# Stacked rows of keys and queries moved in longer and shorter pieces through scratches with gaps, in a cross-attention and sparse-gate kernel on one core

## What is computed

```python
q = (Q @ Wq.T + bq).reshape(B, S, H, D_H).transpose(0, 2, 1, 3)
k = (K @ Wk.T + bk).reshape(B, S, H, D_H).transpose(0, 2, 1, 3)
scores = jnp.einsum('bhqd,bhkd->bhqk', q, k) * inv_sqrt_dh
attn = jax.nn.softmax(scores, axis=-1)
ctx = jnp.einsum('bhqk,bhkd->bhqd', attn, v)
x = x + (ctx.transpose(0, 2, 1, 3).reshape(B, S, D_K) @ Wo.T + bo)   # then x = x + the sparse layer of layernorm(x)
```

## Time and profile before

| | |
|---|---|
| median of three runs | 531.14 us |
| the profiled execution's own time | 530.78 us |
| its span in the profile | 529.0 us |
| outside the span | 1.8 us |
| PE busy over the span | 393.7 us (74%) |
| DVE busy over the span | 411.9 us (78%) |
| DMA queue q1 (SP's), share of the 16 engines over the span | 40.3% |
| packets, and bytes moved | 138970, 53.02 MB |

### The profile page before, as it was taken

The page is one execution under the profiler, slowest core; times in us unless marked ns, Lnnn a source line. Parts: engine busy times, 40 slices in busy tenths (PEclk is TensorE's granted clock), DMA queues, the critical chain, the costliest instruction groups (busy, mean ns, idle before and its releaser), DMA issues.

```text
span 529.0 us, 16337 instructions
## 1 busy us (share of the span) xinstructions
PE 393.7 (74%) x5502; PEld 306.8 (58%) x5516; DVE 411.9 (78%) x1941; ACT 393.8 (74%) x1069; POOL 361.0 (68%) x514
## 2 busy tenths in 40 slices
PE   3455989999999999999897435766685685586543
PEld 1124677777877787777785224555574564465442
DVE  7555566767776877677764299999999999999946
ACT  3414667877887788786675568889999999999863
POOL 7356766788786777865211202569999999989996
PEclk9999988999999999999999556697769768878865
DMA  5787788778878887777500000000000000000011
GB/s 156 160 210 180 164 204 204 182 196 203 186 177 188 189 208 188 188 176 179 124 7 2 0 0 2 1 1 22 22 20 20 22 21 22 21 22 20 22 39 60
DMA packets 138970, 53.02 MB, mean 100 GB/s; under 512 B 105146, under 2 KB 131195, under 8 KB 137339
## 3 DMA queue, kind: packets, MB, share of 16 engines
q1 hardware_dynamic: 136712, 51.47, 40.3%
q10 hardware_dynamic: 2176, 0.52, 0.5%
HBM read 34.67 MB, written 16.78 MB: 97 GB/s over the span
## 4 chain that ended last, share of the span: by engine, by line
SPq 30%; DVE 27%; PE 11%; ACT 9%; DMA 9%; issue 6%; POOL 6%; DVEq 0%; POOLq 0%; ACTq 0%
SPq L295 27%; DVE tops L1050 11%; DVE kst L1062 11%; DMA k_scratch<-k_parts 6%; ACT kst L775 3%; SPq L280 2%; DMA qst<-q_scratch 2%; PE ps_pv L355 2%; POOL kst L1229 1%; ACT kst L786 1%; PE ps_row L530 1%; PE ps_col L340 1%; PE ps_col L530 1%; ACT kst L823 1%; PE ps_row L384 1%
## 5 line engine op out<-in xcount | busy, mean ns | idle before, releaser
L900 DVE TENSOR_REDUCE m<-ps_row 128x8 f32<-128x512 f32 x128 | 82.3, 685 | 53.1 <-PE ps_row L384 53.1
L646 ACT ACTIVATE pT<-ps_col 128x512 f32<-128x512 f32 x128 | 68.6, 588 | 30.3 <-PE ps_col L340 30.3
L1050 DVE MAX8 tops<-kst 128x8 f32<-128x128 f32 x384 | 78.5, 265 | 0.0
L355 PE MATMUL ps_pv<-vx,pT 128*64 128x18 f32 x2048 | 72.8, 213 | 0.0
L355 PEld LDWEIGHTS ps_pv<-vx,pT 128*64 128x64 f32 x2048 | 66.4, 139 | 6.9 <-ACT pT L646 3.5
L1062 DVE MATCH_REPLACE8 kst<-tops,kst 128x128 f32<-128x128 f32 x264 | 69.0, 266 | 0.0
L384 PE MATMUL ps_row<-kst,qst 96*64 96x128 bf16 x1024 | 41.6, 224 | 11.0 <-DMA qst<-q_scratch 11.0
L340 PEld LDWEIGHTS ps_col<-qst,kst 100*128 100x128 bf16 x1024 | 33.9, 99 | 23.9 <-issue 11.5
L340 PE MATMUL ps_col<-qst,kst 100*128 100x64 bf16 x1024 | 41.6, 195 | 7.1 <-DMA qst<-mT 7.1
L558 PE MATMUL ps_pv<-idb,kst 128*128 128x128 bf16 x120 | 10.9, 243 | 42.3 <-ACT kst L786 42.1
L384 PEld LDWEIGHTS ps_row<-kst,qst 96*64 96x64 bf16 x1024 | 32.5, 113 | 14.8 <-DMA qst<-q_scratch 13.1
(11 more groups left out here) (157 smaller groups left out, 1256.3 us busy)
## 6 DMA issues: line engine op xcount, KB each, us to landing
k_scratch<-k_parts SPq DMA_DIRECT2D x32, 192.0 KB, 3.0
q_scratch<-q_parts SPq DMA_DIRECT2D x32, 192.0 KB, 3.0
kst<-k_scratch SPq DMA_DIRECT2D x32, 192.0 KB
qst<-q_scratch SPq DMA_DIRECT2D x32, 192.0 KB
xr<-in_x_dram SPq DMA_DIRECT2D x16, 256.0 KB, 3.9
cT<-in_ctxT_dram SPq DMA_DIRECT2D x16, 256.0 KB, 3.6
kst<-k_scratch SPq DMA_DIRECT2D x32, 128.0 KB
qst<-q_scratch SPq DMA_DIRECT2D x32, 128.0 KB
```

The lines of the kernel that those rows point to most:

```text
L355: mm = pe.matmul(pv_flat[pp * SEQ:(pp + 1) * SEQ, h * 2 * VW:(h + 1) * 2 * VW], pT[:, 2 * j + pp, hh, :], vx[s][:, 2 * hp + pp, h, :], sta ...
L646: act.activation(pT[:, b % PT_RING, :, :], ps_col[b % 2][:, :, :], ACT.Exp, scale=SCALE).then_inc(act_exp, 1)
L900: dve.tensor_reduce(m32[:, b // 4, :, 4 * j:4 * j + 4].rearrange("q a h -> q h a"), ps_row[b % 2][:, :, :, :], AX.X, ALU.max).then_inc(dve ...
L1050: ins = dve.max(top[:, n, :], src)
```

## The change

Keys' stacks get whole rows, zeros included: GpSimd splits the keys into frames (`k_frames`) in which each part already stands between zeros, the scratch write moves these frames (1 KB for one channel and part instead of 512 bytes), and a stacked key row is 16 pieces of 1 KB instead of 64 of 128 bytes. The scratches get a gap of 32 elements (64 bytes) after each channel's row, so that two channels are not adjacent in DRAM; a query row thereby becomes 16 pieces of 512 bytes instead of one of 8 KB. The three memsets of the key stacks go away, and one of `k_frames` (1600 float32 elements per partition instead of 4096 in each of the three) takes the place of the first; SP waits for none of them.

```diff
+GAP = 32
-        k_parts = sb("k_parts", [128, PARTS, GTOK], BF16)
+        k_frames = sb("k_frames", [128, 2 * (PARTS * GTOK + SEQ)], BF16)
-        q_scratch = [nc.dram_tensor(f"q_scratch{s}", (2, PARTS, 128, HALF), BF16).ap() for s in range(2)]
-        k_scratch = [nc.dram_tensor(f"k_scratch{s}", (2, PARTS, 128, HALF), BF16).ap() for s in range(2)]
+        q_scratch = [nc.dram_tensor(f"q_scratch{s}", (2, PARTS, 128, HALF + GAP), BF16).ap() for s in range(2)]
+        k_scratch = [nc.dram_tensor(f"k_scratch{s}", (2, PARTS, 128, GTOK + GAP), BF16).ap() for s in range(2)]
+        k_parts = [k_frames[:, :].rearrange("c (a x) -> c a x", a=2)[:, :, n * GTOK:(n + 1) * GTOK]
+                   .rearrange("c a (p m) -> c a p m", p=PAIRS)[:, :, :, 0:SEQ] for n in range(PARTS)]
...
             for s in range(STACKS):
-
-                if s == 1:
-                    sp.wait_ge(gp_zero, 1)
-                else:
-                    sp.wait_ge(dve_zero, s // 2 + 1)
-                if s == 2:
-                    load_x(2)
                 sp.dma_start(kst[s][MROWS:KROWS, :, :, :, :].rearrange("r h p a m -> r (h p a m)"), minus_rows).then_inc(rows_in, 16)
...
+            load_x(2)
...
                 for a in range(2):
+                    sp.dma_start(k_scratch[s][a, :, :, 0:GTOK].rearrange("n c t -> c n t"),
+                                 k_frames[:, a * PARTS * GTOK:(a + 1) * PARTS * GTOK].rearrange("c (n t) -> c n t", n=PARTS)
+                                 ).then_inc(k_out[s], 16)
...
                     for n in RUNS:
-                        first = PARTS - n if to_keys else 0
-                        src = scratch[s][a, first:first + n].rearrange("n (i h) t -> (n i) (h t)", h=HEADS)
-                        rows = spread(a, n)
-                        dst = (kst[d][rows, :, :, a, :].rearrange("r h p m -> r (h p) m") if to_keys
-                               else qst[d][rows, :, :].rearrange("r h t -> r (h t)"))
-                        if to_keys:
-                            src = src.rearrange("r (x m) -> r x m", m=SEQ)
-                        sp.dma_start(dst, src).then_inc(moved[d], 16)
+                        first = first_part(n)
+                        src = scratch[s][a, first:first + n].rearrange("n (i h) t -> (n i) h t", h=HEADS)
+                        sp.dma_start(stacks[d][spread(a, n)], src[:, :, 0:stacks[d].shape[2]]).then_inc(moved[d], 16)
...
-            dve.memset(kst[0][:, :, :, :, :].bitcast(F32).rearrange("r h p a m -> r (h p a m)"), 0.0).then_inc(dve_zero, 1)
+            dve.memset(k_frames[:, :].bitcast(F32), 0.0).then_inc(dve_zero, 1)
...
-                    dve.memset(kst[2][:, :, :, :, :].bitcast(F32).rearrange("r h p a m -> r (h p a m)"), 0.0).then_inc(dve_zero, 1)
...
+                keys, rest = [b[:, :].rearrange("c (a p m) -> c a p m", a=2, p=PAIRS) for b in (k32, k_rest)]
                 wait(pool, gp_split, 4 * g)
-                pool.tensor_copy(k_parts[:, 2, :], k32[:, :]).then_inc(gp_split, 1)
+                pool.tensor_copy(k_parts[2], keys).then_inc(gp_split, 1)
...
-            pool.memset(kst[1][:, :, :, :, :].bitcast(F32).rearrange("r h p a m -> r (h p a m)"), 0.0).then_inc(gp_zero, 1)
```

More of the change, by code:

```diff
@@ L259, in _, with write_keys @@
             for s in range(STACKS):
-                if s == 1:
-                    sp.wait_ge(gp_zero, 1)
-                else:
-                    sp.wait_ge(dve_zero, s // 2 + 1)
-                if s == 2:
-                    load_x(2)
                 sp.dma_start(kst[s][MROWS:KROWS, :, :, :, :].rearrange("r h p a m -> r (h p a m)"), minus_rows).then_inc(rows_in, 16)
-            def write_parts(g, parts, scratch, done, moved):
+            load_x(2)
+            def write_keys(g):
                 s = g % 2
[L271 to L275, removed]
+                wait(sp, gp_split, 4 * g + 4)
@@ L276, in write_parts @@
                 if g >= 2:
-                    wait(sp, moved[slot(g - 2)], STACK * uses(g - 2))
+                    wait(sp, k_moved[slot(g - 2)], STACK * uses(g - 2))
                 for a in range(2):
-                    sp.dma_start(scratch[s][a].rearrange("n c t -> c n t"),
-                                 parts[:, :, a * HALF:(a + 1) * HALF]).then_inc(done[s], 16)
-            def stack(g, scratch, done, moved, to_keys):
+                    sp.dma_start(k_scratch[s][a, :, :, 0:GTOK].rearrange("n c t -> c n t"),
+                                 k_frames[:, a * PARTS * GTOK:(a + 1) * PARTS * GTOK].rearrange("c (n t) -> c n t", n=PARTS)
+                                 ).then_inc(k_out[s], 16)
@@ new lines, in write_queries, with stack @@
+            def write_queries(g):
+                s = g % 2
+                wait(sp, dve_split, 4 * min(g + 1, 2))
+                wait(sp, gp_qsplit, 4 * (g - 1))
+                if g >= 2:
+                    wait(sp, q_moved[slot(g - 2)], STACK * uses(g - 2))
+                for a in range(2):
+                    sp.dma_start(q_scratch[s][a, :, :, 0:HALF].rearrange("n c t -> c n t"),
+                                 q_parts[:, :, a * HALF:(a + 1) * HALF]).then_inc(q_out[s], 16)
+            def stack(g, scratch, out, moved, stacks, first_part):
@@ L284, in stack @@
                 s, d = g % 2, slot(g)
[L285 removed]
+                wait(sp, out[s], WRITES * (g // 2 + 1))
                 for a in range(2):
                     for n in RUNS:
[L288 to L295 removed]
+                        first = first_part(n)
+                        src = scratch[s][a, first:first + n].rearrange("n (i h) t -> (n i) h t", h=HEADS)
+                        sp.dma_start(stacks[d][spread(a, n)], src[:, :, 0:stacks[d].shape[2]]).then_inc(moved[d], 16)
@@ L297, in _ @@
+            kst_rows = [kst[s][:, :, :, :, :].rearrange("r h p a m -> r h (p a m)") for s in range(STACKS)]
+            qst_rows = [qst[s][:, :, :] for s in range(STACKS)]
             for t in range(FIRST, LAST + 1):
@@ L305, in _ @@
                     wait(sp, pe_col, 8 * (t - 1))
-                    stack(t + 1, k_scratch, k_out, k_moved, True)
-                    stack(t + 1, q_scratch, q_out, q_moved, False)
+                    stack(t + 1, k_scratch, k_out, k_moved, kst_rows, lambda n: PARTS - n)
+                    stack(t + 1, q_scratch, q_out, q_moved, qst_rows, lambda n: 0)
                 if there(t + 2):
-                    write_parts(t + 2, k_parts, k_scratch, k_out, k_moved)
-                    write_parts(t + 2, q_parts, q_scratch, q_out, q_moved)
+                    write_keys(t + 2)
+                    write_queries(t + 2)
             for g in range(GROUPS):
```

9 lines of the change are left out of this document (5 added, 4 removed).

## The result

The changed kernel takes 602.62 us (median of 4 runs, 595.96 to 606.15), the kernel before, timed beside it, 533.89 us: 1.125 times as long, 95% interval 1.1093 to 1.1407 (the ratio leaves out the slowest of the four, which ran in a slower state of the chip). The forecast was 538 us with a range of 520 to 565. It is outside the range, on the slow side. The profiled execution has a span of 594.1 us, against 529.0; it was the fastest of the four (595.96 us), so steps and prices read from it are, if anything, on the short side.

What follows compares the result with a forecast made beforehand. The transfer round (15.1 us a step) was taken as the bound, TensorE (14.5) close behind. New round 15.24 plus 0.3 not covered gave 15.54, +0.46 a step, +7 us over 15 steps: 538 us, range 520 to 565.

Steps and rivals of the forecast that it cites:

- What bounds the kernel before: Attention steps: transfer round 15.1 us, TensorE's work 14.5 us; shorter round gains at most 0.56 us, longer paid in full.
- The keys' stack, 6.4 us: Key stack transfers in a step: 128 pieces of 1 KB on the fullest engines at 50 ns, 6.4 us against 6.14.
- Rival (b): Stack writes crowd each other entering the same partitions: 58 ns per 1 KB piece, step 17.0 us, 560 us; chance 0.33.
- The queries' stack, 3.6 us: Query stack transfers in a step: 128 pieces of 512 bytes per full engine at 28 ns, 3.6 us against 3.93.
- The keys' write, +1.06 us: Keys' scratch write in a step: 48 pieces of 1 KB per engine at 50 ns, 2.4 us against 1.34.
- The sum: Transfer round of a step: key stack 6.4, query stack 3.6, keys' write 2.4, queries' write 1.34, loads 1.5; 15.24 us.
- the 0.3 us not covered: Part of a step outside the transfer round, waiting for the scratch write's landing: 0.3 us kept of 0.83.
- SP should no longer be held back in the keys' stack.: SP's issuing of key stack transfers: with shorter query pieces it is not held there and runs ahead; no size given.
- GpSimd at nothing: GpSimd's split of the keys: same four instructions, ready long before needed, even 1 us more each costs nothing.
- the start between -2 and +2: Kernel start without the memsets: first scratch write issued 2 us earlier but larger; taken as 0, between -2 and +2 us.
- (c): Stack pieces beginning off a boundary cost more, 4 ns each: 1.0 us a step, +15 us, 553 us; chance 0.10.
- (d): Round bound by SP's issuing, not moving: it shrinks below TensorE's 14.52 us a step, 518 to 523 us; chance 0.15.

Runs made afterwards that it cites:

- after_split: Changed kernel with the starts of the 16-row and 8-row transfers exchanged and each 24-row transfer cut in 8 and 16 rows: 556.1 us, 1.040 of the kernel before.

## Why the prediction was wrong, point by point

**What bounds the kernel before.** The round of transfers and TensorE nearly level, with a longer round paid in full: right. The maxima's transfer left out of the kernel before changes nothing, fewer issues of writes change nothing, and a write that is 48 x 47.8 = 2.3 us long instead of 1.34 costs 0.8 to 0.93 us a step.

**The keys' stack, 6.4 us: the step that failed.** The count (128 pieces on the fullest engine) fits and the price was wrong: 78 ns in place of 50, hence 128 x 78 = 10.0 us, +3.6, and 10.1 us is what the stack takes in the trace from its first piece to its last. No trace shows the engine of a packet, but with one piece of 16 KB for a row the first twelve pieces of a stack start together (26.16 to 26.65 us) and the thirteenth only at 27.36, as if 24 rows were dealt to twelve engines; and eight times the price of a row, 8.8 us, is near the 9.3 us that such a stack takes. Why the price was wrong the placements show: the same pieces into other partitions cost from 53 to 115 ns. I had 64 ns as the upper bound, from 44 pieces that load constants, and took the lower value because those stood at a start. Neither row had 1 KB pieces going to rows that lie 4 partitions apart in a few places. Nothing in the line from 512 bytes to 2 KB could show crowding, because both ends use all 128 partitions. Rival (b) had the mechanism, and its own bounds (58 ns, 560 us; all upper bounds, 587 us) were still too low.

**The queries' stack, 3.6 us.** The mean over all 512-byte pieces is 34.1 ns; with the third of them that are writes at 28.4, the stack's cost 37 ns: 4.7 us, +1.1. Without the keys' 1 KB pieces beside them they cost 35, so most of this is not the keys' doing; in the least crowded placement they cost 32.

**The keys' write, +1.06 us.** Right: +0.8 to 0.93 us measured alone, 47.8 ns a piece.

**The sum.** With the measured prices: 10.0 + 4.7 + 2.3 + 1.34 + 1.5 = 19.8 us, against 19.00 measured, so nothing is left over for the 0.3 us not covered. With the crowding taken away (after_split's prices of 53 and 32 ns for the stacks' pieces) it is 6.8 + 4.1 + 2.3 + 1.34 + 1.5 = 16.0 us against 16.57 measured, and 556 us: 538 plus 15 x 0.9 us for these two terms plus the start comes to 553. As a rule for the step the sum is rough, though: the same working gives 27.6 us where the neighbouring rows have 24.95, 20.1 where the kernel without maxima has 18.51, and 17.3 where the one without gaps has 19.61. It counts overlap nowhere, and it has no term for a wait on another queue. What made the forecast wrong was a price from another place; that the rest of the sum came out within 5% in the kernel after is in part luck.

**"SP should no longer be held back in the keys' stack."** Half right: 4.45 us there on average, and only one stack of the sixteen has an issue above 1 us. But SP was held one transfer later, in the queries' stack: 7.3 us on average, 8.74 at most, where I allowed 4.3. The hold had only moved.

**What I did not see at all:** the small transfer of the maxima on another queue. It was late by 1.1 us on average, the first of a group's two by 2.6 us; I had listed it nowhere. It costs 7 to 11 us, if the difference is real.

**GpSimd at nothing, the start between -2 and +2:** right. The four split instructions keep their length to 3% (the two subtractions are 1156 and 1177 ns, before 1162 and 1160), and the start is 1.7 us longer: the first scratch write is issued 2 us earlier, at 12.23, and the stack still starts later.

```profile
12.23 0.96 SPq L276 DMA_DIRECT2D k_scratch<-k_frames  x2
```

**The rivals.** (b) is what happened, at more than its upper price; with a chance of 0.33 for it, the range that ended at 565 left out its upper part. Its sign was half right: 1 KB pieces above 58 ns, but the tens of us of waiting came for the maxima, and for qst's stack there were 6.4 us. (c) is refuted: gaps of 64 and of 256 bytes and none give 602.6, 602.0 and 606.9 us. By the Trainium skill (DMA: Bandwidth & Descriptors, "How a descriptor splits into AXI transactions") the 64-byte gap should have cost extra beats; no run here shows such a cost. (d) is refuted in the form in which I stated it: four times fewer pieces did not shorten the round, fewer issues of writes gain nothing, and with 8 KB query rows SP is held in neither stack and the step is 20.12 us. Two more issues in the queries' stack did cost time, which stays open.

**Do the experiments give a better version?** No. Every kernel that stacks whole key rows moves 0.79 MB more in each stack and 0.39 MB more in each write; the best of them stands at 1.035.

## What to carry to other kernels

A price per piece belongs to the place it goes to: before a price read from one stretch is used for another, compare the partitions of the two, and count how many rows of one transfer lie in the same group of four partitions or 32 apart on the same side of partition 64. Small pieces can hide such crowding: the 128-byte pieces cost 13.0 ns in either placement, the 1 KB pieces did not. And when the engines fill, look at every other transfer on them, however small, and read the last link of the chain as who came last, not as who is at fault, until a run without it says so.

## What the runs showed of the hardware

- The same 1 KB pieces cost 47.8 ns out of all 128 partitions and 51, 59, 68 and 92 ns on average (with the writes in it) for four placements of the same 96 rows (the last with four transfers more); 127 ns in a stretch of the densest.
- A 16 KB row costs 1103 ns, 69 ns for each KB, against 78 ns for the stack's 1 KB pieces, and the kernel is no faster for it (606.9 and 602.6 us).
- A 64-byte or a 256-byte gap between pieces makes no difference (602.6 and 602.0 us).
- 8 KB pieces into the same rows did not get faster with the less crowded placement (450 and 448 ns, and 444 with the 24-row transfers cut), though the 1 KB pieces did.
- Halving the number of issues for the same writes gained nothing (1.002, and 555.8 against 556.1 us); SP waited that much longer for the landing.
- A transfer of 16 KB on another queue lands after 2.4 us on average beside the stacks of the kernel before, after 3.5 us beside those of the kernel after and after 6.4 us beside the most crowded ones; its packets take as long in the first two (19 and 18 ns).
